# Extra matmuls on spare operands in six stretches outside the loops of a transformer-layer kernel

## The reference

```
x = x + attn_a(layernorm(x))   # 16 heads of 128, causal softmax attention, biases, output projection
x = x + ffn(layernorm(x))      # per-token int8 quantisation, 256x256 int8 weight, scale and bias
x = x + attn_b(layernorm(x))   # 16 heads: rotary q, k; 64 slots per head with a running logsumexp,
                               # softmax over slots, gated RMS-normed output, output projection
x = x + ffn(layernorm(x))      # the same weights again
```

## Time and profile before

| | us |
|---|---|
| median of 3 runs | 821.39 |
| lowest, highest | 820.5, 826.27 |
| span of the profiled execution | 819.7 |
| TensorE busy in that span | 770.2 (94%) |

### The profile page before, as it was taken

One profiled execution on the slowest core, in us unless ns is written; L12 is line 12 of the kernel. 1 busy time (PEld: TensorE's weight loads), 2 busy tenths in 40 slices (PEclk: granted clock), 3 DMA queues, 4 the chain that ended last, 5 costly groups with the idle time before them and its releaser, 6 DMA issues.

```text
span 819.7 us, 14465 instructions
## 1 busy us (share of the span) xinstructions
PE 770.2 (94%) x4556; PEld 654.7 (80%) x4556; DVE 581.3 (71%) x1502; ACT 435.4 (53%) x1188; POOL 285.7 (35%) x291
## 2 busy tenths in 40 slices
PE   5899999999999995799999999999999999999963
PEld 4788888888888883478888888888888888888852
DVE  4555555555555558878887888798879888887686
ACT  3555565555556542465556465656564665555420
POOL 6311020201102014444536346355364463553222
PEclk9999999999999999899999999999999999999997
DMA  6110101101010100100101001001010010000001
GB/s 226 40 52 13 38 13 38 51 0 51 13 38 13 51 1 14 53 0 14 54 0 54 10 13 51 0 13 51 0 33 31 13 51 0 13 0 0 1 1 52
DMA packets 23653, 23.74 MB, mean 29 GB/s; under 512 B 2369, under 2 KB 23361, under 8 KB 23506
## 3 DMA queue, kind: packets, MB, share of 16 engines
q1 hardware_dynamic: 23634, 23.51, 9.0%
HBM read 22.45 MB, written 1.05 MB: 29 GB/s over the span
## 4 chain that ended last, share of the span: by engine, by line
PE 90%; DVE 5%; POOL 1%; ACT 1%; issue 1%; DMA 1%; SPq 0%; DVEq 0%; ACTq 0%; POOLq 0%
PE ps L1276 22%; PE ps L1483 11%; PE ps L1385 7%; PE ps L1283 5%; PE ps L1306 5%; PE ps L1349 3%; PE ps L1390 3%; PE ps L1495 3%; PE ps L1520 3%; PE ps L1325 3%; PE ps L1507 2%; PE ps L1402 2%; PE ps L1537 2%; PE ps L1539 2%; PE ps L1509 2%; PE ps L1508 2%
## 5 line engine op out<-in xcount | busy, mean ns | idle before, releaser
L1276 PE MATMUL ps<-xT_hi,w_hi 128*128 128x512 f32 x256 | 110.4, 431 | 5.3 <-DVE rot L1012 3.6
L1276 PE MATMUL ps<-xT_hi,w_lo 128*128 128x512 f32 x256 | 102.0, 399 | 0.0
L1276 PE MATMUL ps<-xT_lo,w_hi 128*128 128x512 f32 x256 | 101.5, 396 | 0.0
L1042 DVE TENSOR_TENSOR wt<-ps,const 128x384 f32<-128x384 f32 x128 | 68.2, 554 | 40.4 <-PE ps L1496 20.4
L383 POOL TENSOR_TENSOR w_lo<-w_raw,w_hi 128x512 fp32r<-128x512 f32 x32 | 40.8, 1285 | 155.8 <-ACT w_hi L535 154.1
L439 POOL TENSOR_TENSOR rot_s<-rot_s,const 128x512 f32<-128x512 f32 x64 | 82.1, 1293 | 21.1 <-ACT rot_s L678 21.1
L580 ACT ACTIVATE wt<-wt,negmax 128x128 f32<-128x128 f32 (+1 forms) x128 | 56.7, 444 | 28.2 <-DVE negmax L906 28.2
L894 DVE TENSOR_TENSOR v<-ps,bv_b 128x256 f32<-128x256 f32 x64 | 27.0, 422 | 51.9 <-PE ps L1283 51.9
L697 ACT ACTIVATE v<-ps 128x256 f32<-128x256 f32 x64 | 24.5, 382 | 72.4 <-PE ps L1483 72.2
L1276 PEld LDWEIGHTS ps<-xT_hi,w_hi 128*128 128x128 f32 x256 | 49.0, 192 | 15.1 <-issue 4.5
L1031 DVE RECIPROCAL enz<-zs 128x128 f32<-128x128 f32 x64 | 60.3, 943 | 1.0 <-ACT zs L684 1.0
(11 more groups left out here) (170 smaller groups left out, 2236.9 us busy)
## 6 DMA issues: line engine op xcount, KB each, us to landing
w_raw<-a_w_q SPq DMA_DIRECT2D x8, 256.0 KB, 2.8
w_raw<-a_w_k SPq DMA_DIRECT2D x8, 256.0 KB, 3.2
wv<-a_w_v SPq DMA_DIRECT2D x8, 256.0 KB, 3.4
wo<-a_w_o SPq DMA_DIRECT2D x8, 256.0 KB, 2.7
w_raw<-b_Wq SPq DMA_DIRECT2D x8, 256.0 KB, 2.7
w_raw<-b_Wk SPq DMA_DIRECT2D x8, 256.0 KB, 3.3
wc<-b_Wv SPq DMA_DIRECT2D x8, 256.0 KB, 3.5
wc<-b_Wg SPq DMA_DIRECT2D x8, 256.0 KB, 3.7
```

Source lines behind the costliest of these rows:

```text
L1042: d.tensor_tensor(dst, src[:, 0:384], tri3, ALU.mult).then_inc(done, 1)
L1276: ins = mm(PJ[n[0]], w[:, m, c, h * P:(h + 1) * P], x[:, c, cols], start=(t == 0), stop=(t == len(terms) - 1))
```

## The change

A helper on TensorE's program issues `count` matmuls of 128 x 128 by 128 x 512 in the rounded float32 form, all into one PSUM bank that nobody reads until it is written anew. It is called in six stretches outside the loops: at the start (13 on the cleared `wo_hi`, then 5 after the first transposes), after `ffn_product(0, 1)` (15), ahead of task k1 of attention B's first pair (9), and in the last pair of attention B ahead of the wait for `og` of batch 2 (8) and of batch 3 (12) and ahead of `ffn_transpose(1, 2)` (10). At the start TensorE waits for a new semaphore, raised by the memset of `wo_hi`, which becomes GpSimd's first of this program rather than its fourth. In batch 2 one wait for bank 5 is added.

```diff
         @block.gpsimd
+            g.memset(wo_hi[:, :, :].bitcast(F32), 0.0).then_inc(warm_ready, 1)
             g.memset(minus_half[:, :], -0.5).then_inc(init_done, 1)
             g.memset(s1[:, :], 0.0).then_inc(init_done, 1)
             g.memset(ws2[:, :], 0.0).then_inc(init_done, 1)
-            g.memset(wo_hi[:, :, :].bitcast(F32), 0.0)
...
+            def keep_busy(bank, source, count):
+                for _ in range(count):
+                    mm(ps[:, bank, :], source[:, 0:P], source, start=True, stop=True)
...
+            cleared = wo_hi[:, :, :].rearrange("p h d -> p (h d)")
+            pe.wait_ge(warm_ready, 1)
+            keep_busy(7, cleared, 13)
             pe.wait_ge(const_ld, 16)
             transpose_x(0, 0, 2)
             transpose_x(0, 1, 3)
+            keep_busy(7, cleared, 5)
             pe.wait_ge(xts[0].lo, 2)
...
             ffn_product(0, 1)
+            keep_busy(4, oT_hi[:, 0, 0, :], 15)
             transpose_x(1, 0, ffns[0].banks[0])
...
+                        if last and b == 2:
+                            pe.wait_ge(b_.proj_evac[2], slot(PAIRS, 0, 2)[1])
+                            keep_busy(5, oT_hi[:, 0, 0, :], 8)
                         pe.wait_ge(b_og, x + b + 1)
...
+                        if last and b == 3:
+                            keep_busy(5, oT_hi[:, 0, 0, :], 12)
                         pe.wait_ge(b_og, x + b + 1)
...
                         if last and b == 3:
+                            keep_busy(5, oT_hi[:, 0, 0, :], 10)
                             ffn_transpose(1, 2, (ffns[1].y, 1))
...
             for j, name in enumerate(B_TASKS):
+                if name == "k1":
+                    keep_busy(4, oT_hi[:, 0, 0, :], 9)
                 b_task(0, 0, j, 0, 0)
```

More of the change, by code:

```diff
@@ L190, in layer_kernel @@
         init_done = sem("init_done")
+        warm_ready = sem("warm_ready")
         ones_done = sem("ones_done")
```

## The result

| | before | changed |
|---|---|---|
| median, us (6 runs each, same chip) | 822.0 | 817.08 |
| lowest, highest | 820.5, 826.27 | 815.65, 818.15 |
| ratio of the two, with its 95% interval | | 0.9933 [0.9914, 0.9953] |
| span of the profiled execution | 819.7 | 816.3 |
| mean granted clock in it | 0.985 | 0.989 |

The change takes 0.67% off; 0.7% was forecast. The interval means 3.9 to 7.1 us, and the two medians of this table differ by 4.9 us. The median of 817.08 lies 1.3 us above the predicted time and inside the range of 812.6 to 819.6. The profiled execution of the changed kernel was the slowest of its six, and it does not show the sum as it was worked out: 3.4 us of the 5.6.

A forecast was written before the change was run, and what follows sets the result against it. TensorE, 94% busy, bounds the loops; outside them its clock drops after waits, and followers' idle time limits the gain. Start 1.8, passage 1.9 and end 1.9 us sum to 5.6 us, giving 815.8 us (range 812.6 to 819.6).

The forecast's parts named there:

- The start's 1.8 us: Up to attention A's loop: k0 starts 1.2 us earlier, held by GpSimd, and a VectorE pause of 0.6 us goes.
- the stop: Before attention A's loop: VectorE's `wt` scaling pauses until GpSimd's bias add ends; its removal was to give 0.6 us.
- if the clock is up by 11.4 us: Premise at the start: q0 and q1 then take 2.8 us instead of 5.19 and end near 14 us.
- The passage's 1.9 us: Between the attentions: VectorE's subtraction 0.5 us earlier, 0.9 from `b_rope_cos`'s wait, 0.5 from its next wait.
- The third term: Between the attentions: VectorE's wait of 0.61 us for GpSimd's rstd was to give 0.5 us.
- The end's 1.9 us: Attention B's last pair: 1.0 us of VectorE idle in batch 2, then 0.3 (FFN product) and 0.6 (`add_y`) in batch 3.
- just enough: Batch 2: `og` transposes and copy, delayed by eight dummies, end near 788.2 us; the out-projection waits until 788.28 anyway.
- transposes don't hold the clock: Rival, passage: the clock falls before the `s1` products, so the first 0.5 us is lost; 816.3 us, chance 0.10.
- the start does not warm: Rival, start: the dummies leave the clock low and net about 0; sum 3.8 us, 817.6 us, chance 0.14.
- dummies hold nothing: Rival, all blocks: the clock moves on something other than matmul activity; no gain, 821.4 us, chance 0.06.
- overrun at the low level: Rival, all blocks: dummies run at the low clock and exceed their cover; 6.2 us lost, 827.6 us, chance 0.03.
- a halved term: Leftover case: one of the forecast's terms comes out at half; said to lie between, with no chance of its own.

The follow-up runs named there:

- e5: Changed kernel with the five dummy blocks behind the start made of float32 transposes instead of matmuls; 816.95 us.
- e7: Changed kernel with 16 instead of 8 dummies ahead of the `og` transposes in batch 2; 817.07 us.
- e8: Changed kernel with mostly larger dummy blocks and small new ones in the other waits outside the loops; 816.02 us.
- e10: Changed kernel with about half as many dummies in each of the five blocks behind the start; 820.03 us.
- e11: The changed kernel timed once more, unaltered; source of its second profile; 816.84 us.
- e1: Changed kernel with only the start's dummy blocks (13 and 5) kept; 821.03 us.
- e2: Changed kernel with only the dummy blocks between the attentions (15 and 9) kept; 822.04 us.
- e3: Changed kernel with only the dummy blocks in attention B's last pair (8, 12 and 10) kept; 820.82 us.
- e6: Changed kernel without the 5 dummies behind the first transposes; 816.84 us.
- e9: Kernel before, without dummies, with GpSimd's bias add on `acc` put ahead of its memset of `accT`; 822.14 us.
- e4: Changed kernel with 7 more dummies ahead of attention A's loop; 816.99 us.

## Why the prediction was right, and where it was not

**The size and the mechanism hold.** The forecast was 5.6 us off the span by three passages of 1.8, 1.9 and 1.9 us. Alone they gave 2.2, 1.2 and 2.4 us by the medians, together 6.1 against 823.2, and 4.9 against the runs that the change was first timed with. The second profile of the changed kernel shows 2.0, 1.5 and 2.6 (the marks at 318.20 and 354.06 taken as the borders). Attention B's loop was forecast to be entered 3.7 us earlier; its mark is 1.58 us earlier in the first profile and 3.49 in the second.

**The start's 1.8 us: right in its parts, wrong in one premise.** k0 did wait for GpSimd's low part. It began at 16.67 before, at 15.57 in the second profile and at 16.18 in the first: 1.1 and 0.5 us, where 1.2 was forecast and TensorE alone would have saved 2.4. From k0 to the loop's first transposes it took 11.09 us before and 10.25 in both profiles, so the stop was worth 0.84 us, not 0.6. 1.1 + 0.84 is the 1.94 of the table, 0.5 + 0.84 its 1.33.

The stop of `wt` went wherever GpSimd was done before VectorE came: in e5, e7, e8, e10 and e11 the bias add ends at 22.9 to 23.2 and the scaling, from 23.3 to 23.6 on, takes 1.0 us instead of 1.93. Where it was not, the second scaling started within 0.01 us of the bias add's end: 25.75 against 25.74 before, 24.39 against 24.38 in e1, 25.37 against 25.36 in e2, 25.68 against 25.68 in e3. In e6, too, both stand at 24.44. e9 corrects the reading: it is not this bias add as such, since a memset in its place does the same. The Trainium skill ("SBUF — State Buffer", "SBUF: two separate sides") says that a VectorE operation in a two-port mode and a GpSimd operation lock the port pair they share for a whole instruction each, and the other blocks; the ends above agree with that.

The step that failed is "if the clock is up by 11.4 us", read as a thing that happens once. In the profiled execution it was up at 6.07, down at 9.48, up at 12.89 and down again at 26.55, and that last stretch, in a loop that TensorE bounds, ate the gain: -1.33 us at the entry had become +0.24 at the q task of the next pair (34.03 against 33.79), and was -0.08 at the passage.

**The passage's 1.9 us: 1.5.** The transposes behind 15 dummies take 0.66 instead of 1.11 us, and VectorE's subtraction comes 0.5 us earlier (327.86 instead of 328.39 at the first maximum of the quantisation). `b_rope_cos` no longer waits its 0.89 us. The third term was mis-sized: the wait of 0.61 us for GpSimd's rstd is there unchanged, since GpSimd's statistics moved with VectorE. The `s1` products ran at the low level again (326.92 to 330.33) and that cost TensorE about 1 us that it would else have waited, as the prediction had it and the rows of e8 bear out.

**The end's 1.9 us: 2.1, and 2.7 in the second profile.** The waits of 0.63, 0.40 and 0.58 us are gone. The lead over before's profile is 1.28 us at 777.55, then 2.00 at 790.89, 2.49 at 792.01, 2.71 at 799.58 (VectorE's FFN step) and 3.37 at 803.20: steps of 0.72, 0.49, 0.22 and 0.66, where the prediction had 0.63, 0.40, 0.3 and 0.58. The cover behind the eight was "just enough": 0.5 us by the rows, 0.4 by e7. Nothing came from the last products, where the clock was low from 808.20 to the end, as written.

**The rivals.** That transposes don't hold the clock fell with e5. The rule of the Trainium skill ("TensorE: Matmul & The Clock Gate", "PE-mode transpose") that stood behind it is not borne out for this kernel's float32 transposes; the rows call them MATMUL and do not tell in which mode the engine runs them. That the start does not warm fell: the clock first rose at 6.07 us, among the matmuls of zeros. That dummies hold nothing, or overrun at the low level, fell by the windows; only the five ran at the low level, in the first profile of the changed kernel (2.48 us, with an overrun of 0.6), in e1 (2.25 us) and in e4 (2.48 us). The test that was written down, no 0.50 ahead of 805 us, failed by a stretch at the start (9.48), one at the entry and one in the passage, and none undid the forecast. The chances of the prediction add up to 1.00 without the case of a halved term that it names behind them, so they leave that case no share.

**What the prediction did not see: the profile of before was a lucky one.** Each execution has its own set of falls. Over the 62 runs of the kernel before that lie beside the experiments (the one of 1958 us is not among them) the mean granted clock is 0.973 to 0.985, and the time goes with it: median 821.2 us at 0.985, 823.4 at 0.979 and 828.6 in the one run at 0.973 (29 runs beside e1 to e4). A line through the 62 has a slope of 4.7 us per 0.01 of clock. One low stretch of 3.41 us lowers the mean by 3.41 x 0.5 / 820 = 0.0021, so by this line it costs 1.0 us on average (an estimate), where TensorE alone would lose 1.7. Before's profile, at 0.985, was at the good end. So the sum of 5.6 was read from a better execution than the one it was set against, and that it meets the 6.1 of the medians within half a us is in part luck: stretches that before's profile did not show can count in the 6.1. How much they do is not separated.

**Open.** The runs don't show what decides in which execution the clock falls at a wait. It is not the length of the wait alone: at the entry of attention A's loop it fell behind waits of 1.76 us (e10), 1.83 (the changed kernel), 2.24 (e1) and 2.34 (e3). It stayed whole through 1.76 (e5), 1.79 (e7) and 1.80 us (e11), and through the longer ones of 2.56 (e9), 2.70 (e2, e6) and 2.71 us (before). The wait of 2.42 to 2.44 us for `qb` in attention A's last pair stands in twelve profiles, and the clock fell there in two of them (e4, e10). What TensorE did ahead of these waits was not varied on its own.

## What to carry to other kernels

When the granted clock shows 0.50 behind waits that can't be removed, matmuls on spare operands into an unread bank can give back what TensorE's followers let through, here 0.7%; size each block to its wait, and put it only where something else is awaited anyway. Sum such a gain by the idle time of the follower, and read the clock of many executions before taking one profile as the typical one. Covering the last gaps brought 0.1% and a narrower spread, not another 0.7%.

## What the runs showed of the hardware

- The clock falls at different waits in different executions of one program, and a stretch that is kept whole at one place often comes back at the next uncovered wait (e4: 26.55 covered, 309.85 low).
- A longer wait is not always the one with the fall. Behind thinned blocks waits of 3.98, 2.69 and 2.38 us were followed by one and one of 1.80 us was not (e10). But at the loop's entry the clock fell behind 1.76 us (e10) and stayed whole through 2.70 us (e6), and waits of 1.83 and 1.80 us there went either way in two executions of the same kernel.
- Matmuls of zeros raise the clock (its first record at 1.00 stands at 6.07 us, with nothing but dummies on the cleared tile before, and at 16.61 us without them), and float32 transposes in the waits behind the start do as well as matmuls (e5: 816.95 against 817.08 us).
- The mean granted clock of a profile counts what lies ahead of the first record as full: the kernel before reads 0.985 though its first twelve matmuls of 512 columns took 0.43 us each.
- VectorE's scaling from SBUF to SBUF stands still until GpSimd's large operation ends: its second operation began 0.00 to 0.01 us behind a bias add in five profiles (before, e1, e2, e3, e6), and its third 0.13 us behind a memset in e9.
